# Local attention with probabilities turned on VectorE in blocks of 32 and a values product on four row groups

## The reference, cut to what matters

```python
def shift_tokens(t):
    a, s = jnp.split(t, 2, -1)
    s = jnp.pad(s, ((0, 0), (1, 0), (0, 0)))[:, :-1]
    return jnp.concatenate([a, s], -1)
def local_attention(q, k, v):          # HEADS 16, DIM_HEAD 64, WINDOW 32
    bk2, bv2 = (look(bk), look(bv))    # this window and the one before it
...
    sim = jnp.einsum('bhwie,bhwje->bhwij', bq, bk2) * QK_SCALE
    sim = jnp.where(mask, -jnp.finfo(sim.dtype).max, sim)
    attn = jax.nn.softmax(sim, -1)
    out = jnp.einsum('bhwij,bhwje->bhwie', attn, bv2)
...
def attn_layer(x, Wqkv, qs, ksc, Wo):
    q, k, v = jnp.split(x @ Wqkv, 3, -1)
    q, k = l2norm(q) * qs, l2norm(k) * ksc      # then rotated
    return local_attention(q, k, v) @ Wo
def ffn_layer(x, g, bln, W1, b1, W2, b2):
    xn = (x - mu) / jnp.sqrt(var + 1e-05) * g + bln
    a, gate = jnp.split(xn @ W1 + b1, 2, -1)
    return a * jax.nn.gelu(gate, approximate=False) @ W2 + b2
for i in range(DEPTH):                 # 6
    x = attn_layer(shift_tokens(x), ...) + x
    x = ffn_layer(shift_tokens(x), ...) + x
```

## Time and profile before

| | us |
|---|---|
| median of 3 runs (lowest, highest) | 4951.03 (4949.79, 4953.73) |
| profiled execution, its own time | 4966.06 |
| its span from first to last instruction | 4964.0 |
| granted TensorE clock, mean over the span | 0.908 |

### The profile page before, as it was taken

The page is one execution under the profiler, slowest core; times in us unless marked ns, Lnnn a source line. Parts: engine busy times, 40 slices in busy tenths (PEclk is TensorE's granted clock), DMA queues, the critical chain, the costliest instruction groups (busy, mean ns, idle before and its releaser), DMA issues. The chain is left out here.

```text
span 4964.0 us, 144956 instructions
## 1 busy us (share of the span) xinstructions
PE 4526.6 (91%) x63640; PEld 3029.1 (61%) x63640; DVE 2875.0 (58%) x3808; ACT 2272.8 (46%) x2592; POOL 2759.3 (56%) x3515
## 2 busy tenths in 40 slices
PE   7799879999999999999757777699999999999997
PEld 3333346776667667766446556367677667767674
DVE  1366157767767776777321112467776777777773
ACT  2255235555555555556210000255555556555553
POOL 0000057777777777777131110377777777777772
PEclk9799989999999999999765555699999999999998
DMA  0000010000000000000000000100000000000000
GB/s 13 5 1 1 4 52 10 10 15 10 2 16 10 15 10 7 2 2 2 7 4 3 3 4 4 51 10 10 7 19 2 16 10 15 10 7 2 2 2 9
DMA packets 14465, 47.84 MB, mean 10 GB/s; under 512 B 3712, under 2 KB 6272, under 8 KB 12032
## 3 DMA queue, kind: packets, MB, share of 16 engines
q1 hardware_dynamic: 13824, 38.42, 2.2%
HBM read 37.37 MB, written 1.05 MB: 8 GB/s over the span
## 5 line engine op out<-in xcount | busy, mean ns | idle before, releaser
L718 POOL TENSOR_TENSOR w_qk<-w_turned 128x1024 f32<-128x1024 f32 x384 | 905.0, 2357 | 115.9 <-DVE w_turned L601 85.1
L596 DVE TENSOR_TENSOR w_turned<-w_ps_qk,w_rot_l 128x1024 f32<-128x1024 f32 x384 | 469.7, 1223 | 715.6 <-ACT w_squares L498 696.2
L255 PE MATMUL w_ps_qk<-w_w_qk,ZT 128*128 128x512 f32 x1536 | 750.6, 612 | 37.8 <-DVE w_turned L601 17.7
L305 PE MATMUL w_ps_y<-w_px,w_w_vo 128*128 128x128 f32 x6144 | 751.1, 276 | 6.9 <-ACT w_px L502 6.7
L305 PEld LDWEIGHTS w_ps_y<-w_px,w_w_vo 128*128 128x128 f32 x6144 | 720.9, 192 | 31.8 <-issue 21.1
L747 POOL TENSOR_TENSOR w_qk<-w_qk,w_inv_norm 128x1024 f32<-128x1024 f32 x384 | 723.2, 1906 | 0.0
L498 ACT ACTIVATE w_squares<-w_ps_qk 128x1024 f32<-128x1024 f32 x384 | 391.6, 1020 | 436.5 <-PE w_ps_qk L255 436.1
L601 DVE TENSOR_TENSOR w_turned<-w_ps_qk,w_rot_l 128x1024 f32<-128x1024 f32 x384 | 466.0, 1213 | 0.0
L605 DVE TENSOR_REDUCE w_sumsq<-w_squares 128x16 f32<-128x1024 f32 x384 | 455.2, 1185 | 0.0
L255 PEld LDWEIGHTS w_ps_qk<-w_w_qk,ZT 128*128 128x128 f32 x1536 | 266.0, 193 | 266.8 <-issue 241.0
L502 ACT ACTIVATE w_px<-w_ps_t 128x1024 f32<-128x1024 f32 x192 | 196.8, 1025 | 505.5 <-PE w_ps_t L297 505.5
(11 more groups left out here) (256 smaller groups left out, 7946.5 us busy)
## 6 DMA issues: line engine op xcount, KB each, us to landing
w_w_qk<-in_w_qk SPq DMA_DIRECT2D x12, 1024.0 KB, 4.8
w_w_vT<-in_w_vT SPq DMA_DIRECT2D x12, 512.0 KB, 3.6
w_w_o<-in_w_o SPq DMA_DIRECT2D x12, 512.0 KB, 5.2
w_w<-in_w SPq DMA_DIRECT2D x12, 384.0 KB, 3.1
w_w<-in_w SPq DMA_DIRECT2D x12, 192.0 KB, 3.1
XT<-in_x SPq DMA_DIRECT2D x1, 1024.0 KB, 4.7
w_rot<-in_rot SPq DMA_DIRECT2D x2, 512.0 KB, 5.8
out<-XT SPq DMA_DIRECT2D x1, 1024.0 KB, 3.9
```

The costliest lines, as they stand in the source:

```text
L255: last = nc.tensor.matmul(ps_qk[:, c, :], Z[:, T.col:T.col + P], w_qk[:, T.parity, cols], start=True, stop=True)
L305: last = nc.tensor.matmul(ps_y[:, D.t * P:(D.t + 1) * P].rearrange("p (a v q) -> p a v q", a=2, q=WIN), w_vo[:, D.parity, h, p, :], px[:, ...
L596: nc.vector.tensor_tensor(turned[:, which, 0, :].rearrange("p (h d) -> p h d", d=DH), flat(ps_qk[:]).rearrange("p (h d) -> p h d", d=DH), ...
L718: nc.gpsimd.tensor_tensor(qk[:, T.odd, which, :], turned[:, which, 0, :], turned[:, which, 1, :], ALU.add).then_inc(pool_add, 1)
```

## The change

The turning of the probabilities moves from TensorE to VectorE: one transpose instruction turns each block of 32 by 32 for itself. A window's probabilities of the 32 keys of the previous window and of the 32 of its own then lie on the partitions of that window's queries, 32 for each window. So the tokens are turned twice instead of four times, once shifted by 32 (`x_tok`), and the values product becomes eight products of 32 rows by 512 columns: four windows on four row groups into four banks, first for the previous window's keys, then, added in PSUM, for the own ones. The four banks are the two of `ps_t` and the two of `ps_s`, now one tensor `ps_w`. The whole values product stands at one place, behind the key projection. With it `place_1` moves ahead of the key projection, the broadcast moves up, VectorE takes the row sums first in its step and has the block transpose ahead of the sum of squares, GpSimd scales the probabilities ahead of its addition, and ScalarE no longer copies `pT`.

```diff
@@ buffers
-        x_win = sb("x_win", [P, TILES * WINS + 2, DIM])
+        x_tok = sb("x_tok", [P, TILES, 2, DIM])
-        pT = sb("pT", [P, PAIRS, P])
-        px = sb("px", [P, 2, 2, 2, PAIRS, WIN])
+        pT = sb("pT", [P, 2, HEADS, WIN])
+        px = sb("px", [P, WINS, HEADS, WIN])
-        ps_t = ps("ps_t", [P, 2, 512])
-        ps_s = ps("ps_s", [P, 2, 512])
+        ps_w = ps("ps_w", [P, 4, 512])
+        ps_t, ps_s = ps_w[:, 0:2, :], ps_w[:, 2:4, :]
@@ TensorE
+            def tokens(B):
+                for half in range(2):
+                    at = B.col - WIN * (1 - half)
+                    last = nc.tensor.transpose(ps_f[:, half * P:(half + 1) * P], Z[:, at:at + P], ident[:])
+                last.then_inc(pe_xt, 1)
-            def turn_probs(C):
...
+            def gather(C):
+                for half in range(2):
+                    for w in range(WINS):
+                        rows = slice(w * WIN, (w + 1) * WIN)
+                        last = nc.tensor.matmul(ps_w[:, w, :], x_tok[rows, C.t, half, :],
+                                                pT[rows, half].rearrange("p h q -> p (h q)"),
+                                                start=half == 0, stop=half == 1)
                 last.then_inc(pe_px, 1)
@@ TensorE, step
-                if D:
-                    if C:
-                        pe.wait_ge(dve_sub, C.n + 1)
-                    gather(D, 1, ps_s)
                 if B:
                     pe.wait_ge(pool_qk, B.n * 2 + 1)
                     if D:
-                        pe.wait_ge(act_px, D.n * 2 + 1)
+                        pe.wait_ge(act_px, D.n * 2 + 2)
                     turn(B, 0, pe_tq)
...
+                place_1(s)
                 if T:
                     pe.wait_ge(dve_turn, T.n * 2 + 1)
                     project(T, 1, pe_k)
-                place_1(s)
                 if C:
                     if B:
                         pe.wait_ge(act_tk, B.n + 1)
-                    pe.wait_ge(pool_p, C.n + 1)
-                    turn_probs(C)
+                    pe.wait_ge(dve_sub, C.n + 1)
+                    pe.wait_ge(dve_pt, C.n + 1)
+                    pe.wait_ge(act_xt, C.n + 1)
+                    gather(C)
                 place_2(s)
                 if B:
                     pe.wait_ge(act_tk, B.n + 1)
-                    if D:
-                        pe.wait_ge(act_px, D.n * 2 + 2)
+                    if C:
+                        pe.wait_ge(act_px, C.n * 2 + 1)
                     scores(B)
                 place_3(s)
-                if C:
-                    pe.wait_ge(act_pt, C.n + 1)
-                    pe.wait_ge(act_xt, C.n + 1)
-                    gather(C, 0, ps_t)
-                place_4(s)
@@ ScalarE
+            def gathered(C, half):
+                pair = slice(2 - 2 * half, 4 - 2 * half)
+                nc.scalar.activation(px[:, pair].rearrange("p w h q -> p (w h q)"), flat(ps_w[:, pair, :]),
                                      ACT.Copy).then_inc(act_px, 1)
@@ VectorE, step (reduce_sum and reciprocal now stand ahead of rotate)
                     rotate(T, 0)
+                if C:
+                    dve.wait_ge(pool_p, C.n + 1)
+                    if D:
+                        dve.wait_ge(pe_px, D.n + 1)
+                    nc.vector.transpose(pT[:].rearrange("p a h q -> p h a q"),
+                                        probs[:].rearrange("p h (a k) -> p h a k", a=2)).then_inc(dve_pt, 1)
                 if T:
                     sum_squares(T, 0)
                 if s.down:
...
@@ GpSimd, step
-                if T:
-                    add(T, B, 0, pe_tq)
                 if C:
                     pool.wait_ge(dve_inv, C.n + 1)
                     nc.gpsimd.tensor_tensor(probs[:], probs[:], spread(row_inv[:], 2, [P, HEADS, KEYS]),
                                             ALU.mult).then_inc(pool_p, 1)
+                if T:
+                    add(T, B, 0, pe_tq)
```

More of the change, by code:

```diff
@@ L263, in turn @@
                 last.then_inc(done, 1)
-            def windows(B, at, count, done):
-                for w in range(count):
-                    last = nc.tensor.transpose(ps_f[:, w * P:(w + 1) * P], Z[:, at + w * WIN:at + w * WIN + P], ident[:])
-                last.then_inc(done, 1)
+            def tokens(B):
[3 more added lines that the diff above has]
+                last.then_inc(pe_xt, 1)
             def scores(B):
@@ L284, in scores @@
                 last.then_inc(pe_s, 1)
-            def turn_probs(C):
-                for p in range(PAIRS):
-                    last = nc.tensor.transpose(ps_t[:, p // 4, (p % 4) * P:(p % 4 + 1) * P],
-                                               probs[:, 2 * p:2 * p + 2, :].rearrange("p h k -> p (h k)"), ident[:])
-                last.then_inc(pe_pt, 1)
-            def gather(C, half, bank):
-                for v in range(2):
-                    w = 2 * half + v
-                    for h in range(2):
-                        rows = slice(h * KEYS, (h + 1) * KEYS)
-                        last = nc.tensor.matmul(
-                            bank[:, h, v * 256:(v + 1) * 256].rearrange("p (a q) -> p a q", q=WIN),
-                            x_win[rows, slot(C, w, h), :], pT[rows, :, w * WIN:(w + 1) * WIN], start=True, stop=True)
+            def gather(C):
[5 more added lines that the diff above has]
+                                                start=half == 0, stop=half == 1)
                 last.then_inc(pe_px, 1)
@@ L377, in place_2 @@
                     merge(layer, parity, quarters[1])
+                elif s.bc:
+                    broadcast(s)
+                if s.B and s.k % TILES == 0:
+                    if s.cen:
+                        pe.wait_ge(act_cen, s.cen.m + 1)
+                    tokens(s.B)
                 if s.gate:
@@ L384, in place_3 @@
                 if s.cen:
+                    if s.B and s.k % TILES == 0:
+                        pe.wait_ge(act_xt, s.B.n + 1)
                     pe.wait_ge(act_cen, s.cen.m + 1)
@@ L389, in place_3 @@
                     last.then_inc(pe_var, 1)
-                if s.bc:
-                    if s.merge():
-                        layer, parity, quarters = s.merge()
-                        pe.wait_ge(act_m, layer * 4 + quarters[1] + 1)
-                    elif s.bias():
-                        layer, parity = s.bias()
-                        pe.wait_ge(dve_bias, layer + 1)
-                    pe.wait_ge(dve_var, s.bc.m + 1)
-                    pe.wait_ge(pool_rstd, s.bc.m + 1)
-                    for t in range(TILES):
-                        last = nc.tensor.matmul(ps_f[:, t * P:(t + 1) * P], rstd[:, t:t + 1].broadcast_to([P, P]),
-                                                ident[:], start=True, stop=True, skip_group_check=True)
-                    last.then_inc(pe_bc, 1)
+                if s.bc and s.merge():
+                    layer, parity, quarters = s.merge()
+                    pe.wait_ge(act_m, layer * 4 + quarters[1] + 1)
+                    broadcast(s)
                 if s.gate:
@@ L406, in place_3, with broadcast @@
                     up(s.up, 2)
-            def place_4(s):
-                if s.B and s.k % TILES == 0:
-                    if s.cen:
-                        pe.wait_ge(dve_var, s.cen.m + 1)
-                    tokens(s)
-                if s.edge:
-                    if s.gate:
-                        pe.wait_ge(act_gate, s.gate.m * FFB + FFB)
-                    elif s.k == 2:
-                        pe.wait_ge(dve_bias, L0 + 1)
-                    else:
-                        pe.wait_ge(act_xt, s.B.n + 1)
-                    windows(s.edge, s.edge.col - 3 * WIN, 2, pe_xe)
+            def broadcast(s):
+                if s.bias():
+                    layer, parity = s.bias()
+                    pe.wait_ge(dve_bias, layer + 1)
+                pe.wait_ge(dve_var, s.bc.m + 1)
+                pe.wait_ge(pool_rstd, s.bc.m + 1)
+                for t in range(TILES):
+                    last = nc.tensor.matmul(ps_f[:, t * P:(t + 1) * P], rstd[:, t:t + 1].broadcast_to([P, P]),
+                                            ident[:], start=True, stop=True, skip_group_check=True)
+                last.then_inc(pe_bc, 1)
             def gate(f, i):
@@ L646, in step @@
                     hidden(s.up, 0)
-                if T:
-                    rotate(T, 1)
-                if s.up:
-                    hidden(s.up, 1)
                 if s.bias():
@@ L655, in step @@
                                             ALU.add).then_inc(dve_bias, 1)
+                if T:
+                    rotate(T, 1)
+                if s.up:
+                    hidden(s.up, 1)
                 if B:
```

79 lines of the change are left out of this document (33 added, 46 removed).

## The result

| | before | after |
|---|---|---|
| median, us | 4952.38 (4 runs, 4949.79 to 4954.68) | 5352.45 (4 runs, 5333.35 to 5360.02) |
| ratio | 1 | 1.080 (95% interval 1.0776 to 1.0826) |
| span of the profiled execution, us | 4964.0 | 5351.2 |
| granted TensorE clock, mean over the span | 0.908 | 0.893 |

The change makes the kernel 8.0% slower, 400 us. The forecast was 5203 us with a range of 5075 to 5400: the direction and the range held, the size came out 150 us short.

A forecast was written before the change was run, and what follows sets the result against it. TensorE's stream bounds the kernel before; after, a ring of waits through the engines. Four steps take 77.4 us against 71.4; 42 x 6.0 = 252 us on 4966.06 gives 5218 profiled, 5203 median, range 5075 to 5400.

The forecast's parts named there:

- The block turning: VectorE's 32 by 32 transpose of the probabilities: taken as 1.2 us, between bounds of 1.02 and 2.36.
- What bounds the kernel: Middle of a windowed stage before the change: TensorE's instruction stream bounds, other engines 2 to 3 us a step short.
- The gather: TensorE's new values product, sixteen passes in four rounds on four row groups side by side: 1.9 us.
- The case of two groups at once: Values product with only two row groups running: about 3.6 us, +286 us, 5489; within dearer unknowns or more clock falls, 0.17.
- The ring, kinds 1, 2, 3: Cross-engine wait path in broadcast, gate and attention-output steps (k not divisible by 4): 17.85, 17.1 and 18.5 us.
- Kind 0: Every fourth step: centring waits for the W2 addition behind VectorE's transpose, TensorE idle 4.6 us; 22.25, with clock loss 23.95.
- The clock: After the centring wait the granted clock falls to 0.50, costing 1.7 us each time; rival without this loss: 5132, chance 0.27.
- The four terms: Lengths of the four successive steps after the change: 17.1 + 17.85 + 18.5 + 23.95 = 77.4 us.
- the 71.4 set for before: Four steps of a batch in the kernel before, at 17.86 us each from the count of rotations.
- The saving on TensorE: TensorE's work falls 1.34 us a step, 225 us; rival that TensorE stays the bound: 4726, chance 0.04.
- PSUM's emptying as the limit: Rule against the change, at ScalarE's copies: scores waiting for both would add 171 us; here they wait for one.
- What to see in the profile: Signs after: centring waits 4 to 5 us every fourth step, values product behind transpose, clock 0.50 stretches, TensorE some 87% busy.

The follow-up runs named there:

- The experiment with both edits: Changed kernel with the W2 addition ahead of VectorE's block transpose and the probabilities scaled ahead of GpSimd's root chain: 4915.5 us, ratio 0.9906 to the kernel before.

## Why the prediction was right, and where it fell short

The block turning, VectorE's group in the kernel after (count, busy us, mean ns, idle time before and what ended it), which the second point uses:

```profile
L603 DVE STREAM_TRANSPOSE w_pT<-w_probs 128x1024 f32<-128x1024 f32 x192 | 239.0, 1245 | 466.0 <-POOL w_probs L732 466.0
```

- **What bounds the kernel.** Right: TensorE was the bound with 2 to 3 us to spare elsewhere, and the change used that up in every kind of step. The middle of the kernel after has no engine above 86%.
- **The block turning.** Taken as 1.2 us between 1.02 and 2.36; the group of all 192, above, has 1.245 us. The sum of squares beside it, of as many elements, took 1.18. By the Trainium skill, Vector Engine (DVE) Microarchitecture Reference, section 3.8, the transpose sustains one element per cycle per lane; the trace agrees as far as it goes, 0.07 us above the reduction.
- **The gather.** Taken as 1.9: 1356.21 to 1358.14 in the kernel after, 1.93. Four row groups run side by side, as in the earlier trace rows. The case of two groups at once (3.6) is out.
- **The ring, kinds 1, 2, 3.** 17.85, 17.1 and 18.5 were forecast; 17.96, 17.23 and 18.41 were measured in the rows above. Scaling ahead of the root chain took their shortest steps to 16.5 to 16.8, about TensorE's own length. That the path runs through the root chain is shown.
- **Kind 0.** 22.25 without and 23.95 with the clock were forecast; 24.02 in the rows above, and 22.33 for the shortest of the experiment with the filled wait, so 1.69 for the clock. The wait was 4.09 us, forecast 4.6. Taking it away gave back 268 us. By kinds: between 1000 and 2000 us the mean kind 0 fell from 24.9 to 18.87 us, (24.9 - 18.87) x 42 = 253.
- **The clock.** Forecast at 1.7 us a kind 0, 71 us; filling the wait gave 77. Of the 13 steps of kind 0 whose first guess lies between 1000 and 2000 us, five took 23.9 to 24.1 us and six took 25.0 to 25.4; in those six the projection took 3.62 us each time, as at 1033.47. The remaining two took 25.62 us (with a pause of 1.3 in the scores) and 27.21 us (a pause of 6.2 ahead of the projection).
- **What failed: the sum has no term for TensorE's stream behind a wait.** The four terms come to 77.4, and the steps without disturbance to 77.62. The mean of four steps is 80.16 in the first stack and 79.88 over both. The 2.26 us between, 95 us in 42 groups, stand in no term. The step of the prediction is the one that put mask and scores at 2.0 us behind ScalarE's copy, 1.02: it priced the wait as its own length and the scores as unbroken. The row of the kernel before already had pauses of up to 0.9 us in the scores with no wait ahead of them; in the kernel after it has 63.7 us against 13.9, so 50 us. The longer stretches at 1.2 GHz are some 1.1 us in 6 of 13 steps of kind 0, 21 us in 42, and the "issue" rows of projection and gather (L251 and L287) have 18 us together against 5. That names 84 of the 95 us, if none of it is hidden. The whole 150 us by which the forecast was short are 109 in these steps (the 95, 9 in the terms and 5 in the 71.4 set for before), 26 in fill, drain and the other layers, which I had counted at nothing and which stay open, and some 14 between profiled executions and medians.
- **The saving on TensorE.** Forecast at 1.34 us a step, 225 us, if TensorE stays the bound. The experiment with both edits bears it out in part: TensorE's busy time falls from 4526.6 to 4317.5 us, 209 us or 1.09 in each of 192 steps, a fifth less than forecast, and the shortest steps of kinds 2 and 3 take 16.48 us, where the shortest before took 16.86 and 17.30, so only 0.4 and 0.8 less. Of the 225 us 42 arrive. 62 went into longer pauses in the scores (76.1 against 13.9), 64 into the wait of the mask products for the copy, which had no such row before, and 49 into the wait of the turning of q and k for ScalarE (L257, 54.5 against 5.4 at L261). These come to 217 us; they are sums over the run, and what of them lies on the path isn't told apart. The pauses cost clock as well: in the 84 steps of each stack it was at 0.50 for 61 us together, against 3.4 in the kernel before, and each of these 16 falls came within 3.6 us after a pause in the scores. Half of the difference, 29 us, is an estimate of what that cost at most.
- **PSUM's emptying as the limit.** One wait of this kind did appear: 56.5 us of the mask products (L269) behind ScalarE's copy, with the pauses that follow it. It is a part of the loss, not the bound. The rule of the Trainium skill, TensorEngine Tiling (Array Packing), PSUM Bottleneck, that emptying PSUM can become the limit, holds here to that extent.
- **What to see in the profile.** The named rows came: centring behind the ZT additions, 4.1 us once in four steps; gather behind the turning; a clock of 0.50 behind the centring wait. TensorE's share in the middle is 86%, forecast 87.

## What to carry to other kernels

Moving work from the bound engine to an idle one pays only if the new order doesn't tie a step that needs nothing of it to the slowest partner: here one addition behind a wait on VectorE, and one order on GpSimd, made a loss of 2.2 us a step where TensorE had saved some 1.1 of busy time, and moving these two gave 437 us back. Before a move, add up the shortest ring of waits through all engines, for each kind of step by itself; here it came out within 0.2 us of the undisturbed steps from rows of the kernel before, and 0.6 us a step below their mean. And a wait of TensorE costs more than its length where a burst of short products stands directly behind it, or where the clock falls: 50 and some 77 us here.

## What the runs showed of the hardware

- A wait directly ahead of the scores' 128 short passes brings pauses of up to 3.4 us in TensorE's stream, at fixed places of the loop, where the same code without it has 0.9 at most: 39.5 us against 13.9 in one kernel, and 18.6 or 10.0 against 76.1 where 1.5 us of mask products or the key projection stand in between.
- Each such pause ends some 2.4 us (2.1 to 3.7 in 296 cases) after a transfer of TensorE's instruction queue began. In the kernel before that transfer begins ahead of the burst, with the added wait inside it in 21 of 22 cases.
- After 4.1 us of idle time the granted clock was 0.50 for some 3 to 7 us; products whose result is overwritten, put into that idle time, made the kernel 77 us faster.
- One VectorE instruction turns 128 x 1024 f32 in blocks of 32 by 32 in 1.245 us, and eight f32 products of 32 rows by 512 columns on four row groups take 1.93 us.
